# Wide attention whose GpSimd forms the low half of the row maxima, and whose row normalisation runs inside the steps

## The reference

```python
xn = (x - mean(x)) / sqrt(var(x) + 1e-5)
q, k, v = split(xn @ w_qkv)                   # 32 heads of 32 columns each
s = (q @ k.T) * 32 ** -0.5                    # 512 x 512 per head
attn = softmax(s)                             # the row maximum is taken off before exp
y = (attn @ v) @ w_out + b_out                # 128 columns
y = (y - mean(y)) / sqrt(var(y) + 1e-6) * ln_gamma + ln_beta
x = x + y
```

## Time and profile before

| | |
|---|---|
| median of 3 runs | 4400.49 us (4398.59 to 4401.84) |
| the profiled execution, its own time | 4390.34 us |
| span of its trace | 4388.6 us |
| mean granted TensorE clock | 0.903 of full speed |
| busy: TensorE, VectorE, ScalarE, GpSimd | 79%, 74%, 56%, 27% of the span |
| wide attention, first load issued to last `y_tok` | 1268.4 to 2564.4 us of the span |
| both normalisation phases, up to the first row of the mixture | 2564.4 to 2622.5 us |

### The profile page before, as it was taken

The page is one execution under the profiler, slowest core; times in us unless marked ns, Lnnn a source line. Parts: engine busy times, 40 slices in busy tenths (PEclk is TensorE's granted clock), DMA queues, the critical chain, the costliest instruction groups (busy, mean ns, idle before and its releaser), DMA issues. The chain is left out here.

```text
span 4388.6 us, 58109 instructions
## 1 busy us (share of the span) xinstructions
PE 3462.0 (79%) x18272; PEld 2099.5 (48%) x18272; DVE 3259.7 (74%) x7326; ACT 2437.3 (56%) x4422; POOL 1191.8 (27%) x734
## 2 busy tenths in 40 slices
PE   5788888678928999999999938792599998656736
PEld 2555555456714445444544416571466665422214
DVE  3999999566846777777777655685388885689986
ACT  2788888445704555555555514571399997312103
POOL 0000000053413555555555524341000000044520
PEclk9899999788958999999999968896799999878768
DMA  5333332113346666665666401341633443000000
GB/s 182 58 64 65 65 45 34 30 51 125 132 94 82 86 83 90 88 84 82 90 89 85 66 31 46 111 146 57 188 57 47 62 60 43 6 20 5 5 28 25
DMA packets 287699, 307.98 MB, mean 70 GB/s; under 512 B 98031, under 2 KB 187567, under 8 KB 287268
## 3 DMA queue, kind: packets, MB, share of 16 engines
q1 hardware_dynamic: 277668, 283.27, 35.9%
q0 software_dynamic: 9728, 20.99, 1.4%
HBM read 124.40 MB, written 78.05 MB: 46 GB/s over the span
## 5 line engine op out<-in xcount | busy, mean ns | idle before, releaser
L1043 DVE TENSOR_REDUCE at_b_top<-ps 128x1 f32<-128x512 f32 x1024 | 662.0, 678 | 325.4 <-PE ps L828 324.0
L957 ACT ACTIVATE at_b_e<-ps 128x512 f32<-128x512 f32 x1024 | 582.2, 598 | 499.3 <-PE ps L834 485.3
L732 POOL TENSOR_TENSOR at_b_e_pair<-at_b_e 128x1024 f32<-128x1024 f32 x256 | 600.9, 2377 | 543.5 <-PE ps L856 473.3
L550 ACT ACTIVATE at_a_e<-at_a_logits,at_a_neg_top 128x512 f32<-128x512 f32 x1024 | 656.1, 716 | 157.5 <-DVE at_a_neg_top L610 155.9
L474 PE MATMUL ps<-at_a_k,at_a_q 96*128 96x512 f32 x1024 | 477.3, 492 | 186.3 <-DVE at_a_clipped L578 117.5
L828 PE MATMUL ps<-at_b_k,at_b_q 96*128 96x512 f32 x1024 | 500.2, 492 | 36.8 <-DMA at_b_k<-at_b_k_hi 33.8
L543 ACT ACTIVATE at_a_eT<-ps 128x512 f32<-128x512 f32 x896 | 461.1, 588 | 0.4
L834 PE MATMUL ps<-at_b_q,at_b_k 98*128 98x512 f32 x1024 | 427.9, 419 | 19.3 <-ACT at_b_e L957 18.9
L606 DVE CUSTOM_DVE_ANT_0 at_a_logits<-ps,at_a_strip 128x512 f32<-128x512 f32 x512 | 340.7, 689 | 110.3 <-issue 33.0
L578 DVE TENSOR_SCALAR at_a_clipped<-ps 128x512 f32<-128x512 f32 x512 | 352.0, 688 | 39.1 <-PE ps L474 38.0
L474 PEld LDWEIGHTS ps<-at_a_k,at_a_q 96*128 96x128 f32 x1024 | 185.2, 190 | 398.8 <-DVE at_a_clipped L578 207.6
(11 more groups left out here) (332 smaller groups left out, 6542.7 us busy)
## 6 DMA issues: line engine op xcount, KB each, us to landing
moe_stage<-in_moe_w SPq DMA_DIRECT2D x46, 768.0 KB
at_b_q<-at_b_q_hi SPq DMA_DIRECT2D x128, 256.0 KB, 5.1
at_b_k<-at_b_k_hi SPq DMA_DIRECT2D x128, 256.0 KB, 7.0
v<-in_a_va SPq DMA_DIRECT2D x64, 256.0 KB, 3.6
at_a_v<-v SPq DMA_DIRECT2D x64, 256.0 KB, 7.1
at_b_q<-at_b_q_lo SPq DMA_DIRECT2D x64, 256.0 KB, 7.6
at_b_k<-at_b_k_lo SPq DMA_DIRECT2D x64, 256.0 KB, 7.3
slot_rows<-empty_slots SPq DMA_DIRECT2D x44, 288.0 KB, 7.1
```

The lines of the kernel that those rows point to most:

```text
L550: act.activation(e[:, j, qb, :], logits[:, j % 2, qb, :], ACT.Exp, bias=neg_top[:, j % 2, qb:qb + 1]).then_inc(exp_done, 1)
L732: pool.tensor_tensor(e_pair[:, j, :, :], e[r][:, j, 0:2, :], e[r][:, j, 2:4, :], ALU.add).then_inc(pair_done, 1)
L957: act.activation(e[r][:, j, b, :], g.ps[:, ST_BANK + b % 2, :], ACT.Exp).then_inc(exp_done, 1)
L1043: dve.tensor_reduce(top[:, t, j, qb:qb + 1], g.ps[:, bank, :], AX_X, ALU.max).then_inc(max_done, 1)
```

## The change

Four things change, all in `attend_wide` and in what follows it.

1. `low_tops` moves from VectorE to GpSimd. It becomes a two-operand `tensor_tensor` subtraction; so that no factor of -1 is needed, both parts now keep their sign and the two rows of `k4` hold -1.0. On GpSimd it stands between the second and the third add of a step (before them in the first two steps, which have no adds).
2. For items 1 to 7 the row normalisation of y and the statistics of the new x run inside the steps c = 6, 7 and 8 that follow the item; for item 8 they run one after another behind the last step. VectorE does `bn_stats` and `bn_aggr` and the scaling (`y_scale`), GpSimd the root (an add of eps and a power of -0.5, both 128x4) and the three two-operand parts of `sum_x` (times gamma, plus beta, plus x; 128x512 each).
3. `y_dram` is no longer written or read, the phase `add_normalised` of this layer and the `row_stats` phase after it are gone.
4. gamma and beta are loaded with the weights, as two broadcast DMAs behind the bias; every engine's first wait covers them. The phase has nine semaphores more.

```diff
-                    pool.memset(k4[r][KROWS:KROWS + 2].bitcast(F32), 1.0).then_inc(set_up, 1)
+                    pool.memset(k4[r][KROWS:KROWS + 2].bitcast(F32), -1.0).then_inc(set_up, 1)
...
+                def root(k, b, moments, mv, eps, rstd, done):
+                    pool.wait_ge(moments, TB * b)
+                    pool.tensor_scalar(var[:, k, :], mv[:, :, 1], eps, None, ALU.add).then_inc(chain, 1)
+                    pool.wait_ge(chain, 4 * (b - 1) + (1 if k == 0 else 4))
+                    pool.tensor_tensor(rstd, var[:, k, :], half[:].to_broadcast([P, TB]), ALU.pow).then_inc(done, 1)
...
+                def sum_x(b):
+                    x = g.x_all[:, (b - 1) * TB:b * TB, :]
+                    pool.wait_ge(y_scaled, TB * b)
+                    pool.tensor_tensor(y_tok[:], y_tok[:], gb[:, 0, None, :].to_broadcast([P, TB, DM]), ALU.mult
+                                       ).then_inc(chain, 1)
+                    pool.wait_ge(chain, 4 * (b - 1) + 2)
+                    pool.tensor_tensor(y_tok[:], y_tok[:], gb[:, 1, None, :].to_broadcast([P, TB, DM]), ALU.add
+                                       ).then_inc(chain, 1)
+                    pool.wait_ge(chain, 4 * (b - 1) + 3)
+                    pool.tensor_tensor(x, x, y_tok[:], ALU.add).then_inc(x_summed, 1)
+
+                def low_tops(st):
+                    n, t = st.n(2), st.slot(2, 2)
+                    pool.wait_ge(hi_done, n)
+                    pool.tensor_tensor(tops[:, 1], top[:, t], tops[:, 0].bitcast(F32), ALU.subtract).then_inc(lo_done, 1)
...
                         for j in range(HG):
+                            if j == 2 and st.has(2):
+                                low_tops(st)
...
+                    if st.i >= 1 and st.c == 6:
+                        root_of_y(st.i)
+                    if st.i >= 1 and st.c == 7:
+                        sum_x(st.i)
+                    if st.i >= 1 and st.c == 8:
+                        root_of_x(st.i)
...
-                    if st.c == 5 and st.has(5):
-                        sp.wait_ge(y_added, st.i)
-                        settle(sp, sp_settled)
-                        sp.dma_start(item(g.y_dram, st.i).rearrange("b p n -> p (b n)"),
-                                     y_tok[:].rearrange("p t d -> p (t d)")).then_inc(y_stored, 16)
...
-                            if (j, qb) == (0, 2) and st.has(2):
-                                low_tops(st)
...
+                                if (j, qb) == (0, 2) and st.c == 6:
+                                    y_stats(st.i)
+                                if (j, qb) == (1, 2) and st.c == 6:
+                                    y_gather(st.i)
+                                if (j, qb) == (1, 2) and st.c == 7:
+                                    y_scale(st.i)
+                                if (j, qb) == (0, 2) and st.c == 8:
+                                    x_stats(st.i)
+                                if (j, qb) == (1, 2) and st.c == 8:
+                                    x_gather(st.i)
...
                 run(dve, step)
+                for part in (y_stats, y_gather, y_scale, x_stats, x_gather):
+                    part(B)
...
-            attend_wide(nc, g, "at_b0", 32 ** -0.5)
-            add_normalised(nc, g, "ln_b0", g.y_dram, a["b0_gamma"], a["b0_beta"], 1e-6)
+            attend_wide(nc, g, "at_b0", 32 ** -0.5, a["b0_gamma"], a["b0_beta"])
+            g.stats_ready = True
```

More of the change, by code:

```diff
@@ L678, in attend_wide @@
         y_tok = ph.sb("y_tok", [P, TB, DM])
+        gb = ph.sb("gb", [P, 2, DM])
+        row_stats = ph.sb("row_stats", [P, 2, TB, 6])
+        y_mv = ph.sb("y_mv", [P, TB, 2])
+        var, y_rstd, half = ph.sb("var", [P, 2, TB]), ph.sb("y_rstd", [P, TB]), ph.sb("half", [P, 1])
+        y_moments, y_root, y_scaled, x_summed, x_moments, x_root, chain, half_set = (
+            ph.sem(k) for k in ("y_moments", "y_root", "y_scaled", "x_summed", "x_moments", "x_root", "chain",
+                                "half_set"))
+        stats_done = [ph.sem(f"stats_done{k}") for k in range(2)]
         sp_settled = ph.sem("sp_settled")
@@ L720, in _, with root_of_y, root_of_x @@
                 for r in range(RQ):
-                    pool.memset(k4[r][KROWS:KROWS + 2].bitcast(F32), 1.0).then_inc(set_up, 1)
+                    pool.memset(k4[r][KROWS:KROWS + 2].bitcast(F32), -1.0).then_inc(set_up, 1)
+                pool.wait_ge(set_up, RQ + 1)
+                pool.memset(half[:], -0.5).then_inc(half_set, 1)
+                pool.wait_ge(half_set, 1)
+                pool.wait_ge(w_loaded, 16 * (U + 4))
+                def root(k, b, moments, mv, eps, rstd, done):
[3 more added lines that the diff above has]
+                    pool.tensor_tensor(rstd, var[:, k, :], half[:].to_broadcast([P, TB]), ALU.pow).then_inc(done, 1)
+                def root_of_y(b):
+                    root(0, b, y_moments, y_mv, 1e-6, y_rstd[:], y_root)
+                def root_of_x(b):
+                    tiles = slice((b - 1) * TB, b * TB)
+                    root(1, b, x_moments, g.mean_var[:, tiles, :], 1e-5, g.rstd[:, tiles], x_root)
+                def sum_x(b):
[12 more added lines that the diff above has]
+                    pool.tensor_tensor(tops[:, 1], top[:, t], tops[:, 0].bitcast(F32), ALU.subtract).then_inc(lo_done, 1)
                 def step(st):
+                    if st.has(2) and not st.has(4):
+                        low_tops(st)
                     if st.has(4):
@@ L740, in step @@
                         pool.tensor_tensor(o_norm[:], o_sb[st.slot(5, 2)][:], r_sb[:], ALU.mult).then_inc(o_done, 1)
+                    if st.i >= 1 and st.c == 6:
[4 more added lines that the diff above has]
+                        root_of_x(st.i)
                 run(pool, step)
+                root_of_y(B)
+                sum_x(B)
+                root_of_x(B)
+                pool.wait_ge(x_root, B)
             @block.sync
@@ L749, in _ @@
                 sp.dma_start(bias[:], g.b_out[None, :].to_broadcast([P, DM])).then_inc(w_loaded, 16)
+                for k, vec in enumerate((gamma, beta)):
+                    sp.dma_start(gb[:, k, :], vec[None, :].to_broadcast([P, DM])).then_inc(w_loaded, 16)
                 def step(st):
@@ L1002, in add_bias, with row_moments, gather_moments, y_stats @@
                     dve.wait_ge(y_ready, U * st.i)
-                    wait(dve, y_stored, 16 * (st.i - 1))
+                    wait(dve, x_summed, st.i - 1)
                     dve.tensor_tensor(y_tok[:], g.ps[:, Y_BANK, :].rearrange("p (t d) -> p t d", t=TB),
                                       bias[:, None, :].to_broadcast([P, TB, DM]), ALU.add).then_inc(y_added, 1)
+                def row_moments(k, b, data):
+                    if k == 0:
+                        dve.wait_ge(y_added, b)
+                    else:
+                        dve.wait_ge(x_summed, b)
+                    for tb in range(TB):
+                        dve.bn_stats(row_stats[:, k, tb, :], data[:, tb, :]).then_inc(stats_done[k], 1)
+                def gather_moments(k, b, mv, done):
+                    dve.wait_ge(stats_done[k], TB * b)
+                    for tb in range(TB):
+                        dve.bn_aggr(mv[:, tb, :], row_stats[:, k, tb, :]).then_inc(done, 1)
+                def y_stats(b):
+                    row_moments(0, b, y_tok)
+                def y_gather(b):
+                    gather_moments(0, b, y_mv, y_moments)
+                def y_scale(b):
+                    dve.wait_ge(y_root, b)
+                    for tb in range(TB):
+                        dve.tensor_scalar(y_tok[:, tb, :], y_tok[:, tb, :], y_mv[:, tb, 0:1], y_rstd[:, tb:tb + 1],
+                                          ALU.subtract, ALU.mult).then_inc(y_scaled, 1)
+                def x_stats(b):
+                    row_moments(1, b, g.x_all[:, (b - 1) * TB:b * TB, :])
+                def x_gather(b):
+                    gather_moments(1, b, g.mean_var[:, (b - 1) * TB:b * TB, :], x_moments)
                 def low(st, bank, hi_done, hi, lo, factor, done):
@@ L1014, in low @@
                                              ALU.subtract).then_inc(done, 1)
[L1016 to L1020, removed]
                 def turn_tops(st):
```

15 lines of the change are left out of this document (7 added, 8 removed).

## The result

| | median, us | runs |
|---|---|---|
| before | 4399.54 | 4 (4398.01 to 4401.84) |
| changed | 4328.35 | 4 (4323.89 to 4329.96) |
| ratio | 0.9844 | 95% interval 0.9829 to 0.9859 |

The change makes the kernel 71 us faster; 4336 was forecast, with 4316 to 4358 as the range. The two profiled executions, 4390.34 and 4327.22 us, are 63.1 us apart; their spans are 4388.6 and 4325.3.

A forecast was written before the change was run, and what follows sets the result against it. TensorE was taken as bounding, idle behind wide attention and losing a few per cent inside to VectorE's stalls. Phases -45.4, steps -20, start +1 sum to -64.4 us: 4400.5 to 4336 us, range 4316 to 4358.

The forecast's parts named there:

- phases that go: Between last `add_bias` and the mixture: 12.6 us of chain and exit replace 58.0 us of idle TensorE, -45.4 us.
- steps: Wide attention: without VectorE's `low_tops` stall, 58 steps of 18.95 us become 18.6, -20 us.
- start: Stage start: two more broadcast loads queue in SP and VectorE waits on the last, +1 us (0.9 to 2).
- The work inside the steps at nothing: Steps c = 6 to 8: added statistics, scaling and GpSimd work fit in slack, cost nothing; at most 19 us in all.
- upper end: Scaling in step c = 7 blocked beside GpSimd, as 7.31 us against 1.12 in layer 6: 9 us, inside those 19.
- The low half at nothing: GpSimd behind its second add: low half done 1.8 us before needed, costs nothing; without that cover up to 0.4 a step.
- The median: Whole kernel: -64.4 us carried over to the median of 4400.5, 10 us above the profiled execution, giving 4336 us.
- Clock stays up: Mixture's router: after only some 15 us idle, TensorE might stay at 2.4 GHz, -11 us, 4325; chance 0.05.
- The wait moves to `turn_tops`: Steps: VectorE waits in `turn_tops` for GpSimd's second add, stall stays, -20 becomes 0, 4356 us; chance 0.04.
- Slower: power is slow: GpSimd's root: a long power routine delays the low half; 12 us loses the gain, 14 us gives 4435; chance 0.03.
- The steps gain nothing: Steps: another wait or the inserted work gives back 19 of the 20 us, 4355; chance 0.14.
- bound by its loads and by TensorE nearly at once: Wide attention without the stall: the k load is late next, so a step takes no less than 18.6 us.

The follow-up runs named there:

- e1: The kernel before with only the low half of the maxima moved to GpSimd: 4360.84 us, ratio 0.9944 to the kernel before.
- e5: The changed kernel with the row statistics of items 1 to 7 computed three times over: 4333.89 us, ratio 0.9884 to the kernel before.
- e3: The changed kernel with the low half behind GpSimd's fourth add instead of its second: 4371.45 us, ratio 0.9974 to the kernel before.
- e7: The kernel before with SP's two q_hi loads issued without waiting for q_lo: 4339.20 us, ratio 0.9902 to the kernel before.
- e2: The changed kernel with the low half back on VectorE, so normalisation only: 4352.73 us, ratio 0.9920 to the kernel before.
- e4: The changed kernel with the root's power executed 12 times instead of once: 4389.34 us, ratio 1.0013 to the kernel before.
- e6: The changed kernel with SP's two q_hi loads issued without waiting for q_lo: 4295.78 us, ratio 0.9795 to the kernel before.

## Why the prediction was right, point by point

| term | forecast | profile | how read |
|---|---|---|---|
| phases that go | -45.4 | -43.4 | 58.04 to 14.65 |
| steps | -20 | -22.8 | first `at_b_xn` to the last `add_bias`, 1287.56 to 1264.77 |
| start | +1 | +1.6 | 8.50 to 10.07 |
| sum | -64.4 | -64.6 | |

That the sum meets the profile to 0.2 us is partly luck: the gain of the phases was forecast 2.0 us too high and the cost of the start 0.6 too low, the gain of the steps 2.8 too low. Each term by itself is right in its mechanism. The spans differ by 63.3: the changed execution came 2.9 us later to the stage, and was 1.6 us shorter behind it; neither place is touched.

- **The phases.** Mis-sized by 2.0 us. The root was taken at 0.7 us from a TENSOR_SCALAR row; it takes 1.35, since a power of 128x4 lasts 1.04 and not 0.36. Twice that is 1.3 of the 2.0 us. The exit took 4.0 where 3.7 was taken, each pair of `bn_stats` and `bn_aggr` x4 1.25 where 1.1 was taken, and the hand-overs the rest. The three parts took 1.26 each, the lower of the two bounds, as chosen.
- **The steps.** 58 steps of 18.58 where 18.6 was forecast, and 1.3 us from the few outside them, which had been left out. That VectorE's stall is a wait for an add, that it is worth the difference between short and long steps, and that the k load is next in line, all stands: e1 gets the whole of it with the low half alone. Short and long stalls were told apart rightly, and the short ones do slip in between two adds; the forecast gave no reason why one does and another doesn't, and none is shown.
- **The work inside the steps at nothing.** Right: steps with c = 6, 7 and 8 take 18.69, 18.57 and 18.58 us in the mean in the changed kernel, and 18.70, 18.57 and 18.57 in e1, which has none of that work in them. For the statistics it is right by the reason given: e5 finds the end of the slack at 1.6 to 1.9 us, where the forecast had 1.9. The scaling, for which the earlier trace rows had been an upper end, takes 7.8 us for the 28 instructions of seven items together, but this is no test of that end: GpSimd has nothing in flight during any of them, while each of the four in the earlier trace rows ran beside a GpSimd instruction. They were not blocked because nothing was there to block them.
- **The low half at nothing.** Right, and only in its place: e3.
- **The start.** 1.6, inside 0.9 to 2.
- **The median.** 4336 was too high by 8 us, and not because of the sum: the 10 us between the profiled execution and the median of before were carried over, and the changed kernel hasn't got them (4327.22 beside 4328.35). The kernel before ranges over 26 us in its runs in all groups, the changed one over 9. That the spread comes of how many stalls are long, which may fall out differently in each run, would fit e7, but no run shows it: e2, which has the stall, kept within 6 us in its four. The forecast's own range, 4322 to 4350, doesn't hold its own lowest case either: 17 us less than 4336 is 4319.
- **The rivals.** "Clock stays up" is refuted by the window of the router (columns as in the earlier trace rows): its clock is 0.50 again, 1.2 GHz, behind 15 us of idleness as behind 60:
```profile
2561.00:2583.00 22.00, 21.03 (x100) 20.28 (x100) 9.78 (x39) 4.78 (x8) 0.76 (x2) 0.50 0.11 36
```
  "The wait moves to `turn_tops`" doesn't happen with the low half behind the second add, and does behind the fourth. "Slower: power is slow" is right in its mechanism and near in its price (e4), but the power takes a twelfth of what it would need. "The steps gain nothing" is refuted by steps of 18.58; it holds only for the normalisation without the low half (e2).
- **What the forecast didn't see** is that "bound by its loads and by TensorE nearly at once" was no floor. The trace of before showed the k load as next in line, and there the reading stopped; what the loads themselves waited for, a semaphore for `q_lo` ahead of transfers that don't need it, was worth 26.6 us more by the medians, 23 of them in the stage.

## What to carry to other kernels

When one instruction's time varies from step to step, look at what runs on the other engine in those microseconds before pricing it at its mean: its mean can be a mixture of short and long waits for that engine, and the long ones may be got rid of by making the steps even as well as by moving the instruction. A transfer that is "next in line" has a start as well as an end: see which semaphore its queue waited on, and whether each transfer behind that wait needs it. A wait that is moved costs in each step what it used to cost in some, so give moved work a place where it is done well ahead of its reader.

## What was not expected of the hardware

A power of four numbers a partition takes 1.02 to 1.04 us on GpSimd, in a row of eleven 0.98 each, where the addition of a constant to the same four takes 0.23 and a subtraction of two 128x16 operands 0.22. The hold-up of a VectorE instruction with two operands in SBUF by GpSimd's adds ends with an add, to 0.04 us, in e7 as in the earlier trace rows. It can be longer than one add: the instruction at 1797.69 in the earlier trace rows takes 3.04 us, and an add lasts 2.38; it waits for the end of the third and then for the whole of the fourth. The Trainium skill, "SBUF — State Buffer", section "Who interferes with whom", states that a VectorE instruction with two SBUF inputs contends with a GpSimd instruction that reads SBUF, and the trace agrees. And the step's loads fill their engines: in one step of the changed kernel 768 packets of 2 KB take 255 ns each in the mean, spread over 16 engines 12.2 of the 18.6 us, and all engines are full from some 4 to 16 us behind the first score. This fits e6, where the first load was issued 1.0 us earlier behind the first score and the last landed 1.1 us earlier.
